# A four-layer graph network on 6,250 nodes: typed rows of 20 node blocks made during the in-degree count, and the edge-feature copy in runs of 6400 bytes

## What is computed

```
src = node_feature[edge_src]
for t in range(3):
    msg = relu(src @ W_e[t].T + b_e[t])          # only where edge_type == t
    parts.append(segment_sum(msg, edge_dst))
agg = concatenate([relu(node_feature)] + parts)
for t in range(3):
    updated = where(node_type == t, agg @ W_n[t].T + b_n[t], updated)
...
deg = segment_sum(ones, dst)                      # in-degree; an out-degree likewise
```

## Time and profile before

| what | value |
|---|---|
| median of 3 runs | 5168.8 us (5166.46 to 5170.2) |
| the profiled execution | 5166.4 us, of which the span is 5164.6 us |
| the count of in-degrees on VectorE | 40.6 to 203.5 us of the span |
| the first stage's end | 239.5 us |
| the slot stage | 266 to 625 us |
| TensorE, VectorE busy over the span | 3645.9 us, 3255.0 us |

### The profile page before, as it was taken

One profiled execution on the slowest core, in us unless ns is written; L12 is line 12 of the kernel. 1 busy time (PEld: TensorE's weight loads), 2 busy tenths in 40 slices (PEclk: granted clock), 3 DMA queues, 4 the chain that ended last, 5 costly groups with the idle time before them and its releaser, 6 DMA issues. The chain is left out here.

```text
span 5164.6 us, 99803 instructions
## 1 busy us (share of the span) xinstructions
PE 3645.9 (71%) x38930; PEld 2640.2 (51%) x38930; DVE 3255.0 (63%) x4527; ACT 1201.7 (23%) x2110; POOL 2201.7 (43%) x2050
## 2 busy tenths in 40 slices
PE   4457755555555555102888887399999599989997
PEld 3345655555555555102777776255555244444444
DVE  7886899999999999202777775766666500230022
ACT  0015655555555555100000000300000200010000
POOL 0051277777777777775777775000000003000300
PEclk9998899999999999656999999699999799989998
DMA  9646799999999999758878777288886367656664
GB/s 315 222 106 226 259 316 334 349 347 344 354 342 345 352 348 345 266 157 156 230 228 229 228 230 181 92 320 305 301 308 250 121 202 228 200 164 201 218 190 138
DMA packets 710790, 1297.10 MB, mean 251 GB/s; under 512 B 367384, under 2 KB 512428, under 8 KB 701260
## 3 DMA queue, kind: packets, MB, share of 16 engines
q1 hardware_dynamic: 579516, 823.86, 49.2%
q10 hardware_dynamic: 60300, 314.88, 15.5%
q0 software_dynamic: 70576, 152.66, 11.7%
HBM read 814.90 MB, written 529.03 MB: 260 GB/s over the span
## 5 line engine op out<-in xcount | busy, mean ns | idle before, releaser
L1394 POOL DMA_INDIRECT big<-typed_msgs,big x1216 | 1374.6, 1130 | 402.4 <-issue 365.7
L1439 PE MATMUL psum<-big 128*128 128x98 bf16 x7936 | 844.9, 206 | 607.3 <-DVE big L1421 567.7
L1439 PEld LDWEIGHTS psum<-big 128*128 128x128 bf16 x7936 | 761.3, 96 | 659.7 <-DVE big L1421 615.1
L2081 PE MATMUL psum<-big 128*128 128x512 bf16 (+1 forms) x4704 | 992.4, 374 | 82.5 <-DMA big<-adj 82.5
L1440 PE MATMUL psum<-big 128*128 128x49 bf16 x7936 | 831.4, 189 | 0.1
L1441 PE MATMUL psum<-big 128*128 128x49 bf16 x7936 | 829.0, 185 | 1.6 <-issue 1.6
L1441 PEld LDWEIGHTS psum<-big 128*128 128x128 bf16 x7936 | 782.0, 99 | 2.2 <-issue 2.1
L2081 PEld LDWEIGHTS psum<-big 128*128 128x128 bf16 x4704 | 460.4, 98 | 606.0 <-DMA big<-adj 83.0
L1440 PEld LDWEIGHTS psum<-big 128*128 128x128 bf16 x7936 | 765.6, 96 | 0.8 <-issue 0.7
L1666 PE MATMUL psum<-big 128*128 128x192 f32 x3648 | 643.8, 331 | 124.1 <-DMA big<-typed_msgs,big 105.1
L1891 PE MATMUL psum<-big 128*128 128x416 f32 x1984 | 656.4, 494 | 63.5 <-DVE big L1925 62.4
(11 more groups left out here) (318 smaller groups left out, 2799.0 us busy)
## 6 DMA issues: line engine op xcount, KB each, us to landing
wadj<-big ACTq DMA_DIRECT2D x248, 784.0 KB
big<-wadj SPq DMA_DIRECT2D x124, 1568.0 KB, 7.0
big<-adj SPq DMA_DIRECT2D x210, 896.0 KB, 4.8
big<-staged SPq DMA_DIRECT2D x304, 384.0 KB, 4.1
staged<-big SPq DMA_DIRECT2D x60, 1920.0 KB
adj<-big ACTq DMA_DIRECT2D x62, 1568.0 KB
big<-edge_feats SPq DMA_DIRECT2D x456, 128.0 KB, 4.2
edge_feats<-in_edge_attr SPq DMA_DIRECT2D x1, 51562.5 KB, 161.6
```

The lines of the kernel that those rows point to most:

```text
L1394: pool.indirect_dma_start(out=sgot4[:, c, u, 0:D], out_offset=None, in_=typed_rows, in_offset=bass.IndirectOffsetOnAxis(ap=pairs4i[:, g, u ...
L1439: pe.matmul(to[:, 0:2 * NB], lo, hi_b[:, q, t, 0:2, 0:NB], start=True, stop=False)
L2081: last = pe.matmul(ps[c % 2][:, 0:len(blocks) * P], terms_[:, k, b * D:(b + 1) * D], ring_a[:, m % RA, 0:len(blocks), s * P:(s + 1) * P], ...
```

## The change

Three things change. The typed-row steps become helpers that both stages call. In the first stage SP waits for `X` before it issues the edge-feature copy, and the copy's access pattern has 4125 x 2 runs of 1600 numbers where it had 880 runs of 15000. And TensorE, ScalarE and SP make and store the typed rows of blocks 0 to 19 (`EARLY = 20`) in the first stage, TensorE in between the counting steps; the slot stage makes those of blocks 20 to 48. The counting loop on TensorE is written out instead of looped. The helpers `turned`, `relus`, `rows_out`, `turn_x`, `messages` and `typed_out` hold what the slot stage's local functions held, moved out of it, with the first block of the stage as a parameter; one of each engine is shown.

```diff
+        EARLY = 20
+        def rows_out(act, b):
+            act.wait_ge(s_z, b + 1)
+            at_least(act, s_mst[b % MZ], 16 * (b // MZ))
+            act.copy(zrows[b % MZ][:, 0:T * D], ps[4][:, 0:T * D]).then_inc(s_ze, 1)
+            act.copy(zrows[b % MZ][:, T * D:KINDS * D].rearrange("p (k c) -> p k c", k=2),
+                     psum[:, 6 * 512:8 * 512].rearrange("p (k c) -> p k c", k=2)[:, :, 0:T * D]).then_inc(s_ze, 1)
...
+        def typed_out(pe, b):
+            pe.wait_ge(s_me, b + 1)
+            at_least(pe, s_ze, 2 * b)
+            for t, to in enumerate((ps[4], ps[6], ps[7])):
+                made = pe.matmul(to[:, 0:T * D], mTs[b % 2][:, t * P:(t + 1) * P], wnT[:, (t + 1) * T * D:(t + 2) * T * D],
+                                 start=True, stop=True)
+            made.then_inc(s_z, 1)
...
 (first stage, SP)
-                sp.dma_start(edge_feats[FRONT:FRONT + E, :], attr).then_inc(s_feats, 16)
+                sp.wait_ge(s_x, 32)
+                assert E % (2 * 25) == 0
+                sp.dma_start(edge_feats[FRONT:FRONT + E, :].rearrange("(a b r) f -> b a (r f)", a=2, r=25),
+                             attr.rearrange("(a b r) f -> b a (r f)", a=2, r=25)).then_inc(s_feats, 16)
...
                 sp.dma_start(edge_pairs[FRONT + MARKS:EROWS, :].rearrange("(p c) r -> p (c r)", p=TAILP), tail_pairs).then_inc(s_pads, 16)
+                for b in range(EARLY):
+                    sp.wait_ge(s_ze, 2 * b + 2)
+                    sp.dma_start(typed_msgs[b * P:(b + 1) * P, :], zrows[b % MZ]).then_inc(s_mst[b % MZ], 16)
                 sp.wait_ge(s_pads, 16 * (5 + -(-width // (U * FE))))
...
 (first stage, ScalarE)
                 act.wait_ge(s_x, 32)
+                for j in range(EARLY + 2):
+                    if j < EARLY:
+                        turned(act, j, 0)
+                    if 1 <= j < EARLY + 1:
+                        relus(act, j - 1, 0)
+                    if j >= 2:
+                        rows_out(act, j - 2)
...
 (first stage, TensorE)
-                in_steps(pe, PAIRS, ins)
-                ins(PAIRS, DST_REST)
+                pe.wait_ge(s_x, 32)
+                done = 0
+                for n in range(HB):
+                    hist_sum(pe, in_count, n, n % 2, opens=n == 0, closes=n == HB - 1)
+                    while done < (n + 1) * (EARLY + 2) // HB:
+                        if done < EARLY:
+                            turn_x(pe, done, 0)
+                        if 1 <= done < EARLY + 1:
+                            messages(pe, done - 1, 0)
+                        if done >= 2:
+                            typed_out(pe, done - 2)
+                        done += 1
...
                 pe.wait_ge(s_end, 1)
+                pe.wait_ge(s_ze, 2 * EARLY)
...
 (slot stage, SP; ScalarE and TensorE take b = EARLY + n in the same way)
-                    if 3 <= n < NB + 3:
-                        b = n - 3
+                    b = EARLY + n - 3
+                    if EARLY <= b < NB:
```

More of the change, by code:

```diff
@@ L376, in along_t, with turned, relus, turn_x @@
             return v.rearrange("p (g t) -> p g t", t=TU).unsqueeze(2).to_broadcast([P, TG, n, TU])
+        EARLY = 20
+        def turned(act, b, b0):
+            act.wait_ge(s_xT, b + 1)
+            if b >= b0 + 2:
+                act.wait_ge(s_m, b - 1)
+            act.copy(xTs[b % 2], ps[2][:, 0:P]).then_inc(s_xTe, 1)
+        def relus(act, b, b0):
+            act.wait_ge(s_m, b + 1)
+            if b >= b0 + 2:
+                act.wait_ge(s_z, b - 1)
+            for t in range(T):
+                made = act.activation(mTs[b % 2][:, t * P:(t + 1) * P], ps[3][:, t * P:(t + 1) * P], ACT.Relu,
+                                      bias=beT[:, t:t + 1])
+            made.then_inc(s_me, 1)
+        def rows_out(act, b):
[4 more added lines that the diff above has]
+                     psum[:, 6 * 512:8 * 512].rearrange("p (k c) -> p k c", k=2)[:, :, 0:T * D]).then_inc(s_ze, 1)
+        def turn_x(pe, b, b0):
+            if b > b0:
+                pe.wait_ge(s_xTe, b)
+            pe.transpose(ps[2][:, 0:P], X[:, b * D:(b + 1) * D], ident).then_inc(s_xT, 1)
+        def messages(pe, b, b0):
+            pe.wait_ge(s_xTe, b + 1)
+            if b > b0:
+                pe.wait_ge(s_me, b)
+            for t in range(T):
+                made = pe.matmul(ps[3][:, t * P:(t + 1) * P], weT[:, t * D:(t + 1) * D], xTs[b % 2], start=True, stop=True)
+            made.then_inc(s_m, 1)
+        def typed_out(pe, b):
[5 more added lines that the diff above has]
+            made.then_inc(s_z, 1)
         in_count = ps[5][:, 0:NB]
@@ L1143, in store @@
                     act.copy(tabs[:, k, 0:3, :], ps[k][:, 0:3 * SLOTS].rearrange("p (r g) -> p r g", r=3)).then_inc(s_slot_e, 1)
[L1145 to L1163, removed]
                 for n in range(GB + 1):
@@ L1169, in _ @@
                         store(n - 1)
[L1170 to L1175, removed]
+                    b = EARLY + n
+                    if EARLY <= b - 1 < NB:
+                        turned(act, b - 1, EARLY)
+                    if EARLY <= b - 2 < NB:
+                        relus(act, b - 2, EARLY)
+                    if EARLY <= b - 3 < NB:
+                        rows_out(act, b - 3)
             @block.tensor
@@ L1181, in outs @@
                         hist_sum(pe, out_count, HB + j, (HB + j) % 2, opens=j == 0, closes=j == HB - 1)
[L1182 to L1199, removed]
                 outs(0, AHEAD)
@@ L1203, in _ @@
                     k = n % 2
-                    if n < NB:
-                        turn(n)
+                    b = EARLY + n
+                    if b < NB:
+                        turn_x(pe, b, EARLY)
                     pe.wait_ge(s_sb_st, n + 1)
@@ L1211, in _ @@
                     last.then_inc(s_slot_T, 1)
[L1212 to L1215, removed]
+                    if EARLY <= b - 1 < NB:
+                        messages(pe, b - 1, EARLY)
+                    if EARLY <= b - 2 < NB:
+                        typed_out(pe, b - 2)
                     outs(*shares[n])
```

## The result

The changed kernel takes 5324.28 us (median of 4 runs, 5315.53 to 5327.15), the kernel before 5169.5 us beside it (4 runs). The ratio is 1.0301, 95% interval 1.0288 to 1.0313: 155 us slower. The profiled execution took 5327.15 us with a span of 5325.4, 160.8 more than the span before.

What follows compares the result with a forecast made beforehand. VectorE was taken to bound the count, TensorE the slot loop. The count ends 161 us later, less 15.8 gained: net 145 on 5166.4, then 2.4 for the median, gives 5314 us; range 5255 to 5355.

Steps and rivals of the forecast that it cites:

- The order in SP's queue: First stage, SP's queue: what is issued behind the copy stays behind it, and issues are held until the copy makes room.
- The rival that the stores overtake the copy: SP's queue: shorter runs let stores pass, no stall, only bursts paid, 24 us more, 5193 us; chance 0.08.
- Where the stall begins: Count: block 3's `typed_out`, behind counting step 28, waits for block 2's copy and store 0; stall from about 86 us.
- The copy's length: Edge-feature copy on SP's queue: 174 us with runs of 6400 B, 8% over 161.6, landing at 209.
- The rival of 15 engines: Edge-feature copy runs on 15 of 16 engines: 186 us, 12 later, 5326 us; chance 0.27.
- The store's landing: Store 0, behind the copy on SP's queue: lands one usual store time, 5.2 us, after it, at 214.
- The count's rest: Count after store 0 lands: 1.2 + 2.6 + 0.95, 71 steps for 114.3, bursts 31; ends at 364 us.
- The burst term: Count behind the restart: each burst costs B - 1.3, taken as 2.1 us; 15 bursts, 31 us (22 to 42).
- My cold row: TensorE's messages and rows after an idle stretch: 3.83 us at granted clock 0.74, 4.1 with a transpose.
- The gain: Slot loop: twenty steps go from 3.85 to 3.06 us, 15.8 us less.
- The wait for X, the written-out code: First stage: SP's wait for `X` costs nothing; loading TensorE's written-out code beside the copy is priced at nothing.

Runs made afterwards that it cites:

- the fastest version: Changed kernel with early stores on ScalarE's queue and typed work in 100 pieces between counting steps; ratios 0.9977 and 0.9979 to the kernel before.

## Why the prediction was right, point by point

**The order in SP's queue.** Right, and it is the point that decided: with the stores on another queue the stall was gone. But what held the store was, for all but its last 9.0 us, the issue. The prediction says that issues are held until the copy makes room, and its sum then lets the store wait in the queue for the copy's landing; in the trace SP was held in the first `marks` issue up to 183.1 and came to the store at 198.6. So the three small packets in 130 us say little about the order of what has been issued. The trace before says more: there the third of the seven `marks` issues begins at 35.98, so two pieces had been issued by then, and no small packet moved in 50 to 150. The Trainium skill (page "DMA: Bandwidth & Descriptors", section "Queues, rings and completion order") says that one engine's ring is consumed in order, and the trace before agrees, by these rows. In the changed kernel's trace 72 packets under 2 KB moved in 185 to 190, ahead of the copy's landing at 203.5; the views sum over the 16 engines and don't tell whether those engines still had parts of the copy. The rival that the stores overtake the copy fell.

**Where the stall begins.** The wait stood where it was placed: block 2's copy, block 3's `typed_out`, behind step 28. Forecast 86 us and a few more; VectorE stopped at 101.8 (213.51 - 111.69). The difference is the two steps that VectorE is ahead (3.2), four bursts ahead of the stall (167.8 - 111.7 - 45.2 = 10.9 us), and a count that begins 1.4 us later, at 42.06: 86 and these are 101.5. None of it matters, as the end of the stall is set by the store.

**The copy's length.** Forecast 174 us, measured 168.0, so a landing at 209 became one at 203.5. (The profile counts the length from the issue's start, 34.1, and the forecast added it to the issue's end, 34.8; after the change the issue began at 35.55.) The 8% by packet size was 4%. The rival of 15 engines was right about the engines and wrong about the time. The share fell from 1.02 to 0.93, which is 15 of 16, and 4000 and 4400 outer entries brought it back to 0.99 and 1.01. The Trainium skill (same page, section "Why a DMA increments its semaphore by 16 and not by 1") has that rule, the largest divisor up to 16, and the trace agrees. But I had priced it at 16/15 of the time, because the engines had been busy throughout; the run with 4000 entries shows 328 GB/s on 16, and packets that take 0.308 us instead of 0.290. A busy share of 1.0 was read as "the engines are the limit", and that was the mistake of that rival: an engine counts as busy also while its packet is slow.

**The store's landing.** Forecast 5.2 us behind the copy, measured 4.1 (203.5 to 207.6). The restart of TensorE's count was forecast for 217.8 and took place at 212.42: 6.4 us earlier by the landing, 0.8 later because the typed rows of block 3 held TensorE for 3.42 us (209.00 to 212.42) where 2.6 was taken, and 0.2 for ScalarE's copies.

**The count's rest.** The number of steps, 71, was right: the trace has 30 of VectorE's before the stall and 71 behind it. **The burst term was mis-sized**: forecast 31 us (22 to 42) for 15 bursts, measured 45.2. The rule for the cost was right: a burst costs what it holds TensorE less 1.3 us. (The terms given for it, 0.77, 0.95 and 0.1 against 3.22, leave 1.4; the trace gives 1.3: held 4.11, lost 2.83; held 5.37, 76.79 to 82.16, lost 4.07.) What was too small is the time for which TensorE was held. I took the middle between warm, 2.75, and cold, 4.1, on the argument that TensorE is half idle between bursts; by the rule, 3.0 lost per burst means 4.3 held on the mean, above what I had for cold. My cold row came from a window at 0.74 and so was itself half warm; at a granted 0.51 a burst took 5.2 us (87.40 to 92.58, before the stall). By the same rule 15 bursts at 2.75 would lose 22 us, so about half of the 45.2 is laid to the lower clock; that is an estimate, no run had all its bursts at the upper level. The count ended at 374.5 where 364 was forecast: 14.2 more for the waits, 1.5 more for the pace of the steps between them, and 5.2 less for the restart.

**The gain.** Forecast 15.8 us, measured 14.3 as changed, and 14.6 (360.3 against 345.7) between the kernel without early rows and the one with the stores on ScalarE's queue, on one chip. That is 0.71 to 0.73 us a step on the mean, where the one step that I read gave 0.79.

**The wait for X, the written-out code.** Costed at nothing, and that held: 1.0007 (0.9991 to 1.0023) without early rows.

**Sum.** 145 us forecast, 160.8 measured between the two profiled executions and 154.8 between the medians; 5314 against 5324.28. The mechanism was right, the closeness is partly luck: the landing came 6.4 us too late in the sum and the bursts 14.2 too cheap, which partly cancel, and the median lies 2.9 us under the profiled execution where I had put it 2.4 above.

## What to carry to other kernels

Before work is moved into an idle stretch of an engine, ask where its output's DMA stands: a store that an engine has to issue behind a long copy ended with the copy here, at runs of 6400 and of 6000 B, and a ring of two or three buffers then carries that wait back to every engine. Put it on a queue without such a transfer, and keep the long copy's runs short enough that the other queue's stores keep up. And measure a filler against the slack of one step of the loop that it goes into, not against the loop's total idle time: the same work cost 58 us in 20 bursts and nothing in 100 pieces.

## What the runs showed of the hardware that was not expected

- The copy from DRAM to DRAM went at 325 and 327 GB/s on 15 DMA engines and at 328 on 16, with the same 6400 B runs and the engines in use nearly all busy. A packet took 0.290 us on 15 and 0.308 on 16. With 6000 B runs on 16 engines it was 314. When stores from on-chip memory ran beside it, all together reached 361, so 16 engines can carry more than the copy alone moved; what limited the copy stays open.
- An issue behind a long copy can hold the engine that makes it: one DMA of 128 KB took 146.44 us to issue behind the copy of 8250 runs, and the seven small ones took 125.08 us behind that of 880. This, more than the order among DMAs that had been issued, delayed the stores.
- A second queue gets in between a copy's packets, and its latency goes with the length of these: stores of 576 KB kept up with runs of 6400 B (no wait for them of over 2.2 us in the two runs of the fastest version), and landed only every 27 to 29 us beside runs of 60 KB (from 104 to 188 us).
- The counting step on TensorE (16 matmuls of 49 columns) takes 0.95 us at the upper and at the lower level of the clock. In 100 to 160 us the kernel before had 592 of these matmuls, 35.39 us busy, at a granted clock of 1.00, and the kernel without early rows 597, 35.51 us busy, at 0.50. The typed rows do depend on it, 0.89 against 1.62 us for one part. So a low clock can be there unseen and is paid for only by the new work.
- The level at which the count starts differed between two executions of the same changed kernel: 0.50 in 40 to 60 us in the one shown above, 1.00 in the other, with TensorE idle for 7.5 us ahead of its last work before the count in both. It did not matter: in both the stall's 98 us from 107 to 205 are at 0.50, and the 15 bursts behind it cost 45.2 and 46.0 us. With pieces in every gap the level was 1.00 (56 of 60 us busy with the stores on ScalarE's queue, 74.7 of 80 with them on SP's), in the second case after 105 idle us at 0.50 (100 to 205).
